# A two-layer adapter and expert kernel: the first layer wholly in 16-bit parts, bias in the gated product, full rows in the adapter step

## What is computed

```python
# layer 0: masked softmax pooling, then ALL experts on all tokens
logits = einsum('bld,ed->ble', x, gate_weight)
kth    = sort(logits.reshape(-1))[expert_k - 1]     # a threshold over all 16384
gates  = logits * (logits >= kth)
h      = gelu(einsum('bld,ehd->bleh', x, w1) + b1)  # x: the pooled tokens
y      = einsum('bleh,edh->blde', h, w2) + b2
x      = x + einsum('blde,ble->bld', y, gates)
# layer 1: an adapter chosen by the sequence's language
h      = relu(x @ W1[lang] + b1[lang])
x2     = layernorm(x + h @ W2[lang] + b2[lang]) * gamma + beta
n      = layernorm(x2) ; probs = softmax(n @ gate_w) ; top 2 of 8 experts
x      = x + x2 + sum over the 2 experts of weight * (gelu(n @ w1 + b1) @ w2 + b2)
```

## Time and profile before

| | us |
|---|---|
| median of 3 runs | 413.64 (412.56 to 415.41) |
| the profiled execution | 413.44 |
| its span in the profile | 411.6 |
| TensorE busy | 384.4 (93%) |
| ScalarE busy | 213.2 (52%) |
| VectorE busy | 194.7 (47%) |
| GpSimd busy | 174.1 (42%) |

### The profile page before, as it was taken

The page is one execution under the profiler, slowest core; times in us unless marked ns, Lnnn a source line. Parts: engine busy times, 40 slices in busy tenths (PEclk is TensorE's granted clock), DMA queues, the critical chain, the costliest instruction groups (busy, mean ns, idle before and its releaser), DMA issues.

```text
span 411.6 us, 6974 instructions
## 1 busy us (share of the span) xinstructions
PE 384.4 (93%) x2005; PEld 245.4 (60%) x2005; DVE 194.7 (47%) x679; ACT 213.2 (52%) x373; POOL 174.1 (42%) x172
## 2 busy tenths in 40 slices
PE   6789999999999999999999988969999899899993
PEld 5667765565555555666666655537888787344441
DVE  0556324455512241463774866315799983223521
ACT  1064345454554343366567446438698997334430
POOL 3055200000003876742478166752175330488833
PEclk9699999999999999999999899989999999999998
DMA  7758696220007633222354011121244427242211
GB/s 225 220 155 272 182 390 254 57 54 2 0 6 190 147 90 114 83 76 78 84 154 125 25 37 38 51 84 30 79 132 143 116 72 185 56 81 54 63 35 51
DMA packets 49296, 44.15 MB, mean 107 GB/s; under 512 B 7244, under 2 KB 40420, under 8 KB 49132
## 3 DMA queue, kind: packets, MB, share of 16 engines
q1 hardware_dynamic: 45240, 37.77, 31.8%
q0 software_dynamic: 2688, 5.25, 4.4%
q10 hardware_dynamic: 1332, 0.69, 0.7%
HBM read 32.02 MB, written 11.67 MB: 106 GB/s over the span
## 4 chain that ended last, share of the span: by engine, by line
PE 71%; DVE 8%; issue 5%; POOL 5%; DMA 4%; SPq 2%; ACT 1%; ACTq 1%; POOLq 0%; DVEq 0%
PE bank L620 28%; PE bank L573 8%; PE bank L574 7%; PE bank L575 7%; POOL sorted_in L1637 3%; PE bank L987 2%; DMA vm<-in_vm 2%; DVE l L669 2%; PE bank L1259 2%; PE bank L1258 2%; PE bank L937 2%; DMA sorted_out<-yo 1%; SPq L762 1%; PE bank L1219 1%; PE bank L550 1%
## 5 line engine op out<-in xcount | busy, mean ns | idle before, releaser
L643 ACT ACTIVATE h<-bank,b1f 128x512 f32<-128x512 f32 x160 | 109.7, 687 | 141.3 <-PE bank L620 138.6
L620 PE MATMUL bank<-h,w 128*128 128x512 f32 x320 | 164.7, 598 | 1.9 <-DVE yo L1700 1.9
L738 POOL TENSOR_TENSOR acc<-acc,tmp 128x512 f32<-128x512 f32 x52 | 70.9, 1364 | 112.5 <-DVE tmp L709 104.3
L573 PE MATMUL bank<-xh,wh 128*128 128x512 f32 x128 | 87.0, 680 | 0.0
L620 PEld LDWEIGHTS bank<-h,w 128*128 128x128 f32 x320 | 60.3, 191 | 18.9 <-DVE yo L1700 2.4
L709 DVE TENSOR_TENSOR tmp<-bank,Gs 128x512 f32<-128x512 f32 x28 | 19.3, 688 | 67.7 <-PE bank L620 67.6
L574 PE MATMUL bank<-xl,wh 128*128 128x512 f32 x128 | 51.3, 401 | 0.0
L575 PE MATMUL bank<-xh,wl 128*128 128x512 f32 x128 | 50.9, 398 | 0.0
L573 PEld LDWEIGHTS bank<-xh,wh 128*128 128x128 f32 x128 | 24.4, 190 | 30.5 <-issue 17.5
L574 PEld LDWEIGHTS bank<-xl,wh 128*128 128x128 f32 x128 | 24.5, 192 | 19.0 <-issue 19.0
L637 ACT ACTIVATE h<-bank,b1f 128x256 f32<-128x256 f32 x76 | 31.6, 478 | 5.3 <-PE bank L552 4.0
(11 more groups left out here) (203 smaller groups left out, 564.5 us busy)
## 6 DMA issues: line engine op xcount, KB each, us to landing
Gs<-gates SPq DMA_DIRECT2D x40, 256.0 KB, 5.2
sorted_in<-zer SPq DMA_DIRECT2D x14, 448.0 KB, 4.4
w<-in_w SPq DMA_DIRECT2D x16, 256.0 KB, 3.8
wraw<-in_w SPq DMA_DIRECT2D x8, 512.0 KB, 3.7
wraw<-sorted_in SPq DMA_DIRECT2D x19, 128.0 KB, 2.2
sorted_out<-yo SPq DMA_DIRECT2D x19, 128.0 KB, 1.9
wh<-in_w POOLq DMA_DIRECT2D x8, 256.0 KB, 4.1
wraw<-in_w SPq DMA_DIRECT2D x8, 256.0 KB, 3.3
```

What stands on the lines that cost most here:

```text
L573: pe.matmul(o[:, :], w_h, a, start=True, stop=False)
L620: pe.matmul(o[:, :], w2[:, e, c * 128:c * 128 + 128], h32[:, u % NH, :], start=(c == 0), stop=(c == 3))\
L643: act.activation(h32[:, u % NH, :], bank[u % 4][:, :], ACT.Gelu if layer else ACT.Gelu_apprx_tanh, bias=b1f[layer][:, e * 4 + c:e * 4 + c ...
L738: pool.tensor_tensor(a, a, tmp[:, i % NTMP, :], ALU.add).then_inc(s_acc, 1)
```

## The change

In words:

1. **Layer 0's second matrix in two fp16 parts.** `FULL` lists the quarters c that stay one fp32 product: none in layer 0, 0 and 2 in the last group. All others are *split*: `hi_part`, `lo_part` and three products of 128x512 take the place of one fp32 product. `pe_m2` waits for the low part, and so does the GELU that reuses the buffer. High parts go alternately to ScalarE (odd units) and VectorE (even units) in layer 0 (`SHARE0` 0.5), and to ScalarE alone in the last group (`SHARE1` 1.0); for tiles nothing changes. The positions are those of the tiles: the high part at u (VectorE) or u + 0.7 (ScalarE), the low part at u + 1.4 on VectorE. `AT` is unchanged.
2. **Layer 0's first matrix in fp16.** `xh`, `xl`, `wh`, `wl` become fp16, with scales 256 and 64 that the GELU's scale undoes. The scores' fp32r helpers get a buffer of their own.
3. **Layer-0 weights.** One load of 1024 columns per expert; `scale_w` multiplies it by 64, `high_w` casts both halves, `low_w` subtracts both. ScalarE scales and casts expert 0 (ahead of the exponents), GpSimd does all the rest. Expert 0's load moves ahead of the tokens' load on SP.
4. **Bias b2** is added in the gated product on VectorE (`scalar_tensor_tensor` with a column of `b2T`), so five matmuls, five copies, five additions and the loads of the gates for them go.
5. **Full rows in the adapter step.** `cw2` and `hTs` are padded with zeros to 128 rows.
6. **Last group.** SP loads quarters 0 and 2 of the second matrix, and GpSimd scales them (eight instructions over 256 columns during the tiles).

The core of the diff:

```diff
+XP = 256.0
+FULL = [(), (0, 2)]
-SHARE = 0.75
+SHARE, SHARE0, SHARE1 = 0.75, 0.5, 1.0
...
-        xh = sb("xh", [128, 2, N // 2], F32R)
-        xl = sb("xl", [128, 2, N // 2], F32R)
+        xh = sb("xh", [128, 2, N // 2], F16)
+        xl = sb("xl", [128, 2, N // 2], F16)
...
-        cw2 = sb("cw2", [A + 1, B, D])
+        cw2 = sb("cw2", [128, B, D])
-        hTs = sb("hTs", [A + 1, 512])
+        hTs = sb("hTs", [128, 512])
...
+        def is_split(u):
+            kind, v, c = UNITS[u]
+            return kind == "tile" or c not in FULL[STEPS[v][0]]
+        def act_share(u):
+            return SHARE0 if u < US else SHARE if u < UD else SHARE1
+        HIA = [SPLIT[u] and int(nsp[u] * act_share(u)) > int((nsp[u] - 1) * act_share(u)) for u in range(NU)]
...
-                if kind == "dense":
+                if SPLIT[u]:
+                    pe.wait_ge(s_lo, nsp[u])
+                else:
                     pe.wait_ge(s_g, u + 1)
...
+                a, b_ = h16[:, u % NH, :], l16[:, u % NH, :]
+                pe.matmul(o[:, :], w_h, a, start=(c == 0), stop=False)
+                pe.matmul(o[:, :], w_l, a, start=False, stop=False)
+                pe.matmul(o[:, :], w_h, b_, start=False, stop=(c == 3)).then_inc(s_m2, 1)
...
-                if NH <= u < US + NH or u >= UD + NH:
+                if u >= NH and SPLIT[u - NH]:
+                    act.wait_ge(s_lo, nsp[u - NH])
+                elif u >= NH:
                     act.wait_ge(s_m2, u - NH + 1)
...
-            if UNITS[u][0] == "dense":
+            if not SPLIT[u]:
                 continue
             if HIA[u]:
                 at("act", u + AT["hia"], hi_part("act", u))
             else:
                 at("dve", u, hi_part("dve", u))
             at("dve", u + AT["lo"], lo_part(u))
...
-                dve.tensor_tensor(o, src, Gs[:, j % NGS, :], ALU.mult).then_inc(s_tmp, 1)
+                dve.scalar_tensor_tensor(o, src, b2T[layer][:, e:e + 1], Gs[:, j % NGS, :], ALU.add, ALU.mult)\
+                    .then_inc(s_tmp, 1)
...
+        def scale_w(k):
+            def fn(eng):
+                eng.wait_ge(s_raw[k % 2], loaded(k))
+                raw = wraw[:, k % 2, :]
+                if k == 0:
+                    eng.activation(raw, raw, ACT.Copy, scale=WS).then_inc(s_ws, 1)
                 else:
+                    eng.tensor_scalar(raw, raw, WS, None, ALU.mult).then_inc(s_ws, 1)
...
+            def by_pool(pool):
+                pool.wait_ge(s_ws, k + 1)
+                pool.tensor_copy(wh[:, k, :], raw[:, 0:512])
+                pool.tensor_copy(w2h, w2r).then_inc(s_wh, 1)
...
             def fn(pool):
+                pool.wait_ge(s_wh, k + 1)
+                pool.tensor_tensor(wl[:, k, :], raw[:, 0:512], wh[:, k, :], ALU.subtract).then_inc(s_w, 1)
+                if NF:
+                    pool.tensor_scalar(w2[:, k, 0:NF * 128], raw[:, 512:512 + NF * 128], HS, None, ALU.mult)
+                pool.tensor_tensor(w2l, w2r, w2h, ALU.subtract).then_inc(s_wv, 1)
...
+                at("act" if k == 0 else "pool", EX[0] - 0.5 if k == 0 else w_free(k) + 0.1, scale_w(k))
+                at("act" if k == 0 else "pool", EX[0] - 0.4 if k == 0 else w_free(k) + 0.2, high_w(k))
+                at("pool", w_free(k) + 0.3, low_w(k))
...
+        def scale_w2b(e):
+            def fn(pool):
+                pool.wait_ge(s_w2b, 16 * (e + 1))
+                pool.tensor_scalar(w2[:, e, 0:256], w2[:, e, 0:256], WS * HS, None, ALU.mult).then_inc(s_w2f, 1)
...
             load_x(sp, 1)
+            load_w(0)(sp)
             sp.dma_start(xtm[:, :, 0:D], t["xtm"]).then_inc(ld["xtm"], 16)
...
-        for v in b2_order:
-            at("pe", mpos[("b2", v)], b2_mm(v))
```

More of the change, by code:

```diff
@@ L137, in build_adaln_ffn @@
     UNITS += [("dense", s, c) for s in range(NS0, NS0 + E) for c in range(4)]
+    SPL0 = [c for c in range(4) if c not in FULL[0]]
+    NF = len(FULL[0])
     NU = len(UNITS)
@@ L312, in build_adaln_ffn @@
         s_w = sem("s_w")
-        s_wd = [sem(f"s_wd{i}") for i in range(2)]
+        s_ws = sem("s_ws")
+        s_wh = sem("s_wh")
+        s_wv = sem("s_wv")
         s_w16h = sem("s_w16h")
@@ L316, in build_adaln_ffn @@
         s_w2b = sem("s_w2b")
+        s_w2f = sem("s_w2f")
         t_rk = sem("t_rk")
@@ L339, in build_adaln_ffn @@
         s_scr1 = [sem(f"s_scr1_{g}") for g in range(NG)]
-        s_gtb = [sem(f"s_gtb{i}") for i in range(1 + NG)]
+        s_gtb = [sem(f"s_gtb{i}") for i in range(GA)]
         s_out = sem("s_out")
@@ L1653, in build_adaln_ffn, with dve_b2 @@
         at("dve", 60.2, dve_fgs)
+        def dve_b2(dve):
+            for i in range(2):
+                dve.wait_ge(ld[f"b2T{i}"], 16)
+                last = dve.tensor_scalar(b2T[i][:, :], b2T[i][:, :], WS * HS, None, ALU.mult)
+            link(dve, "dve", last)
+        at("dve", 50.3, dve_b2)
         def tile(i):
@@ L1877 @@
     x = i["x"].reshape(N, D)
+    order = list(FULL[0]) + [k for k in range(4) if k not in FULL[0]]
     a = {
```

163 lines of the change are left out of this document (85 added, 78 removed).

## The result

The changed kernel takes **449.7 us** (median of four runs, 448.7 to 452.2) against 414.5 (four runs, 412.6 to 419.4): 1.088 of the time before, 95% interval 1.084 to 1.092. The forecast was 435 in a range of 402 to 458, slower by over 1% with a chance of 0.69. The sign and the range held; the most likely value was 15 us too low, and the time lies outside the 424 to 446 to which the forecast had given 0.52. The profiled execution has a span of 450.0 and lasted 452.2. Each group of experiments ran beside the kernel before, whose median there was 414.4 to 416.8.

A forecast was written before the change was run, and what follows sets the result against it. TensorE was taken to set the pace before, with VectorE's added parts, its queue order and waits for GpSimd outweighing TensorE's savings: 2 + 10 + 10 - 1.5 + 3 + 3 - 1 - 4 = +21.5, about 435 us, range 402 to 458.

The forecast's parts named there:

- Start, first stage: Start to 57.5 us: earlier weight load +2; VectorE's parts held by GpSimd's weight preparation +10 (-3 to +18).
- the term for GpSimd's scaling: 32 to 57.5 us: scaling 1024 columns taken as 1.1 us, upper bound 2.5; 4.9 us an expert, 34 for seven.
- Bisection: 57.5 to 115 us, 17 rounds: VectorE's order makes a round 3.85 us instead of 3.24; +10 (8 to 16).
- The rival of a falling clock: Bisection: TensorE's clock falls to 1.2 GHz, 23 us more, 458 in total; chance 0.05.
- 115 to 128.7 us: Nine units: free of the bisection, -2.5, but first kept product waits for the gates' load: -1.5.
- Kept stage: 128.7 to 157.1 us, kept results added: VectorE and GpSimd exclude each other, 29 to 33 us; +3, if not exclusive -8.
- Adapter 0 to the tiles: 157.1 to 243.7 us: TensorE 68, VectorE 76 to 97 against 86.6, +3 (-10 to +10); 243.7 to 271.1 us: -1.
- its term for the waits: 157.1 to 243.7 us: VectorE held by GpSimd, 106 instructions x 0.37 x 0.6 us, 20 us more at the most.
- Tiles and last group: After 271.1 us: adapter step -1.6, new GpSimd scalings +1, last group -3.4 - 1, gather hides about 1; together -4.
- The pair: Adapter step: 33-row pair takes 0.42 us, eight 3.4 a group; full rows about 1.8, saving 1.6 a group.
- Full exclusion with slow GpSimd passes: First stage +18, bisection +15, kept +5, long stage +10: +44, 457 in total; chance 0.12.

The follow-up runs named there:

- narrow additions: Changed kernel with GpSimd's additions of the first layer's 32 expert results made for 32 of 512 columns; 428.5 us, 1.022 of before.
- the second profile: The changed kernel run once more, unchanged, for a second profile; 448.2 us.
- the fp32 kernel: Changed kernel with the first layer's second matrix back in fp32 (all four quarters), all else of the change kept; 393.5 us, 0.947 of before.
- narrow parts: Changed kernel with low parts made for 32 of 512 columns in units 4 to 127 of the first layer; 404.7 us, 0.966 of before.
- more slack in the order: Changed kernel with six buffers in place of four and the second-matrix products two units later in TensorE's order; 429.4 us, 1.035 of before.
- half the units split: Changed kernel with quarters 0 and 2 of the first layer's second matrix in fp32, 1 and 3 split; 420.4 us, 1.010 of before.
- the run with 33 rows: Kernel with the first layer's second matrix in fp32, adapter step's second product with 33 rows again in place of 128; 403.4 us, 0.967 of before.

## Why the forecast was right, and where it was wrong

**Start, first stage: right in size, partly by luck.** +12.5 against +12. Casts and low parts are held as I said, and the groups of 20 to 72 us in the changed kernel show it (busy, mean ns of one | idle before):

```profile
L848 POOL TENSOR_SCALAR wraw<-wraw 128x1024 f32<-128x1024 f32 x7 | 20.2, 2880 | 0.1
L867 POOL CAST w<-wraw 128x512 f16<-128x512 f32 x7 | 5.0, 714 | 0.0
L866 POOL CAST whl<-wraw 128x512 f16<-128x512 f32 x7 | 4.6, 663 | 0.5
...
L702 DVE SCALAR_TENSOR_TENSOR l<-h 128x512 f16<-128x512 f32 x10 | 9.0, 904 | 0.0
...
L691 DVE TENSOR_SCALAR h<-h 128x512 f16<-128x512 f32 x6 | 4.5, 748 | 7.4 <-PE bank L654 4.7 <-ACT h L676 2.7
```

A low part takes 0.90 in the mean where a free one takes 0.68, a high part 0.75 instead of 0.42. But the term for GpSimd's scaling was mis-sized: 2.88 us for 1024 columns where I took 1.1 from the memset and set 2.5 as the upper bound. With the casts at 0.66 to 0.71 (0.6 taken) an expert costs 6.7 us, not 4.9, and the weights were ready at 70.5 us. That I still met the number comes of two further errors. VectorE's low parts were mostly not held beside the scaling, as these rows of the timeline show (a high part of 0.77 us, 0.35 more than a free one, and a low part of 0.68, as a free one, inside a scaling; a low part of 1.63 beside two subtractions):

```profile
35.96 2.77 POOL L848 TENSOR_SCALAR wraw<-wraw 128x1024 f32<-128x1024 f32 x1
36.51 0.77 DVE L691 TENSOR_SCALAR h<-h 128x512 f16<-128x512 f32 x1 [1.70 <-ACT h L676]
...
38.10 0.68 DVE L702 SCALAR_TENSOR_TENSOR l<-h 128x512 f16<-128x512 f32 x1
...
40.30 1.20 POOL L876 TENSOR_TENSOR whl<-wraw,whl 128x512 f16<-128x512 f32 x1
40.41 1.63 DVE L702 SCALAR_TENSOR_TENSOR l<-h 128x512 f16<-128x512 f32 x1
41.46 1.60 POOL L879 TENSOR_TENSOR w<-wraw,w 128x512 f16<-128x512 f32 x1
```

And TensorE, waiting, lost its clock, which I had looked for only in the bisection:

```profile
40.00:45.00 5.00, 2.25 (x11) 1.99 (x10) 4.90 (x10) 1.48 (x3) 4.91 (x4) 0.81 0.15 29
45.00:50.00 5.00, 3.91 (x13) 1.87 (x11) 1.42 (x4) 1.07 (x2) 4.85 (x6) 0.50 0.19 78
50.00:55.00 5.00, 4.32 (x15) 2.85 (x16) 2.52 (x7) 1.31 (x2) 4.85 (x5) 0.50 0.35 105
```

It was busy for 2.25 of the 5 us in which the clock fell, and its 28 products of the next 10 us ran at 1.2 GHz. From 30 us to the first sum it worked for 15.3 us at half the clock, which is worth up to 7.6 of the 12.5 us. This term stood nowhere in my sum for the stage, and the same program with less of it had the first sum 7.5 us earlier; so that +12 was met is luck to that extent. By the Trainium skill ("GPSIMD Engine Reference", Engine selection) one-input GpSimd work runs roughly at line rate; for the casts the trace roughly agrees (0.66 to 0.71 us for 512 columns, where ScalarE took 0.63), for the scaling it does not (2.88 us for 1024), and the measurement decides.

**Bisection: the number right, the chain wrong.** Forecast 3.85 us a round, measured 3.77 to 3.80; +9.1 against +10. I had put both low parts and the counts in front of the sum. In the trace only the odd low part is in the chain, and what I had as three products behind it are nine; the four terms in front of the sum also add up to 3.03 us, where I wrote 2.95. Moving that one part in the order brought 8.2 us of the 9.1 back. The rival of a falling clock fell: the stage runs at 1.00 throughout.

**115 to 128.7 us:** -0.1 instead of -1.5; nothing rests on it.

**Kept stage: the mechanism right, the time 1 to 5 us too long.** Forecast 29 to 33 us by adding VectorE's and GpSimd's work because they exclude each other; measured 27.9, VectorE busy without a break. It stayed the same length as before (28.4), where I had +3. Its groups there, in the changed kernel and then with narrow additions:

```profile
L770 POOL TENSOR_TENSOR acc<-acc,tmp 128x512 f32<-128x512 f32 x11 | 17.1, 1551 | 90.5 <-DVE tmp L743 90.1
L702 DVE SCALAR_TENSOR_TENSOR l<-h 128x512 f16<-128x512 f32 x13 | 11.9, 926 | 0.0
...
L691 DVE TENSOR_SCALAR h<-h 128x512 f16<-128x512 f32 x7 | 7.4, 1054 | 0.0
```

```profile
L702 DVE SCALAR_TENSOR_TENSOR l<-h 128x512 f16<-128x512 f32 x14 | 9.6, 696 | 0.0
L771 POOL TENSOR_TENSOR acc<-acc,tmp 128x32 f32<-128x32 f32 x12 | 7.4, 620 | 82.1 <-DVE tmp L743 82.0
...
L691 DVE TENSOR_SCALAR h<-h 128x512 f16<-128x512 f32 x7 | 3.0, 430 | 0.0
```

With GpSimd's additions short, high parts fall from 1054 to 430 ns, low parts from 926 to 696, and the stage from 27.9 to 18.7 us. This is the exclusion of the earlier trace rows, now shown by an experiment: a high part of 0.42 us waited 0.6 us in the mean. The Trainium skill ("Advanced Engine Details and Errata", GPSIMD Details) ties this conflict to 2-port modes and two SBUF inputs; the trace agrees in that the gated products from PSUM kept 740 ns in both, while those of kept results, with two inputs in SBUF, fell from 866 to 741.

**Adapter 0 to the tiles: the step that failed.** I had added up each engine's work, 68 us for TensorE and 76 to 97 for VectorE in the stretch that ended at 243.7, and took the larger sum as its length (its term for the waits, 106 x 0.37 x 0.6, is 24 us and not 20, which changes nothing here). The corresponding stretch of the changed kernel:

```profile
178.10:286.70 108.60, 80.31 (x361) 38.54 (x362) 87.34 (x242) 58.98 (x91) 66.61 (x47) 0.87 0.29 73
```

VectorE was busy 87.3 us, inside my 76 to 97. But the stage took 108.6. The sum of the busiest engine is only a lower bound when three queues in fixed order wait for each other; in the bisection I had followed the order, here I had not. Two sorts of waits make up the difference. The first, in time (the changed kernel, one row of each engine):

```profile
193.36 6.44 POOL L770 TENSOR_TENSOR acc<-acc,tmp 128x512 f32<-128x512 f32 x3
...
202.68 0.87 DVE L1319 BATCH_NORM_STATS2 st<-x 128x6 f32<-128x128 f32 x4 [5.42 <-POOL x L1369]
...
204.60 0.61 PE L652 MATMUL bank<-h,w 128*128 128x512 f16 x1 [4.77 <-DVE l L702]
```

Three additions of GpSimd, 1.27 us each, took 6.44 because VectorE's parts came between; GpSimd's scaling and shift of group 0 stood behind them; VectorE's statistics waited 5.4 us for these, and the low parts stood behind the statistics; TensorE waited 4.8. The waits of TensorE in this stretch, adapter 0 to 2 (us in total, times, longest):

```profile
PE bank L652 <- DVE l L702: 12.1, 6, 4.8
PE bank L1288 <- POOL acc L770: 11.2, 3, 6.3
PE bank L652 <- DVE tmp L743: 1.0, 1, 1.0
```

24 us in the profile's account, as much as TensorE's whole idle time there (80.2 - 57.4 = 22.8); before, the stretch had none. The second line is the adapter's first product waiting for GpSimd's late additions; behind it in TensorE's queue stand the products that VectorE and ScalarE would work on next. And after such waits the clock fell, which lengthened the products that followed:

```profile
200.00:210.00 10.00, 5.40 (x15) 2.51 (x16) 7.29 (x18) 2.75 (x4) 8.36 (x7) 0.68 0.17 43
```

From adapter 0 to the tiles the clock was at half for 31 us, and TensorE was busy for 23.5 of them (28 and 19.6 in the second profile; 3.4 and 3.4 in the fp32 kernel). Half of that busy time is the most that it can have cost: up to 10 of the 28 us between the two kernels, 8 of 25 in the second profile. How much of it lay on the path no run separates from the waits that brought it on.

The experiments bear the waits out in three ways: VectorE's time for low parts is worth nearly its full length there (25 us for narrow parts, up to 7 of them by the clock), more slack in the order returns 5 to 8 us, and shorter additions of GpSimd 7 to 10 (77.1 or 80.1 to 70.3 from adapter 0 to 2). With half the units split the clock stays at 1.00 from adapter 0 to 2, and TensorE is idle for 62.7 - 54.3 = 8.4 us of the stretch, against 0.7 with fp32. The profile names 5.5 us of waits there, mostly the same two (low parts 2.8, late additions 2.2); what the other 3 are I did not find.

**Tiles and last group:** -5.8 against -4, the adapter rows among it. The pair takes 0.22 us instead of 0.42, as forecast; the run with 33 rows had a fall of the clock behind one of the four groups of pairs, worth about as much again. This I had left out; it may be part of why the fp32 kernel is 20 us faster than before where I had expected 13. Another part: a first-layer unit with fp32 second matrix now takes 0.65 + 0.86 = 1.51 us instead of the 1.57 of the earlier trace rows, from the first matrix's 16-bit parts (3.04 us a bisection round instead of 3.23).

**Rivals.** Full exclusion with slow GpSimd passes (457) came nearest in time, but its parts did not: its large terms were the first stage and the bisection, which came as in the forecast. TensorE's products did become cheaper, as the diff says; with VectorE's parts in front of them that was worth nothing until the last group.

## What to carry to other kernels

Before moving work from a full engine to a half-idle one, follow one round of every stage through the queues in their order; the larger of two busy sums is a lower bound, and here it was 21 us short. An added step in front of the engine that sets the pace is paid in full where it stands behind something that itself waits, so ask of each place what it is queued behind. The useful part of this change was the rest of it (bias in the gated product, full rows, the first matrix in fp16, the last group's parts): with the second matrix left in fp32 it is 5% faster than before. Of these only the full rows were tested alone. And look at the granted clock of a stage before you put its time down to an edit: the same program had its first bisection sum anywhere from 67.6 to 75.1 us.

## What was not expected of the hardware

- A GpSimd scaling of 1024 fp32 columns took 2.77 us and more, 2.88 in the mean, a cast of 512 from fp32 to 16 bits 0.66 to 0.71 in the mean, a subtraction of 512 1.17 to 1.27. Per column the one-input scaling costs 2.8 ns, more than the two-input subtraction's 2.3 to 2.5, and twice the cast. It held VectorE less often than the others: in the changed kernel the three low parts beside it alone took 0.68 us each, as if free, and a high part 0.77 instead of 0.42, while low parts beside two subtractions took 1.63. But in two other kernels a low part inside a scaling took 1.23 (all high parts on ScalarE) and 1.54 (half fp32).
- An addition over 32 columns on GpSimd took 0.24 us at the least, but 0.62 in the mean beside a busy VectorE.
- TensorE's granted clock can fall behind a stretch in which the profile has TensorE busy throughout. It did so behind 33-row pairs twice, at 185 us in the fp32 kernel with 33 rows (0.87 over 13 us) and at 228 us in the kernel before, but not behind the other six groups of such pairs in the two; behind the four groups with 128 rows in the fp32 kernel it never did. That is a hint, not a proof.
- Kernels with the same program up to the first bisection sum differed by up to 7.5 us there, while one kernel repeated to 0.4 us. The time at half the clock in that stage differed with it, 3.4 to 17 us. What sets the clock off stays open.
